# A gathered double-weight kernel: the first slot of x issued first, cond moved to ScalarE's queue, 2 MB of x ahead of the hold

## The reference

```python
def reference(x, subjects, conditions, weights0, weights1):
    x = x + einsum('bct,bcd->bdt', x, weights0[subjects])
    x = x + einsum('bct,bcd->bdt', x, weights1[conditions])
    return x
```

## Time and profile before

| What | Value |
|---|---|
| time, median of 3 runs | 92.88 us (92.86 to 92.94) |
| time of the profiled execution | 92.97 us |
| its span, first to last instruction | 91.2 us |
| TensorE busy (matmuls) | 79.2 us, 87% |
| VectorE, ScalarE busy | 61.8 us, 58.6 us |
| DMA moved | 35.93 MB, mean 394 GB/s |
| DMA queue q1 (SP's) | 33.56 MB, 91.5% of 16 engines |
| DMA queue q0 (the gather) | 2.10 MB, 5.4% |
| DMA queue q10 (ScalarE's) | 0.13 MB, 0.5% |

### The profile page before, as it was taken

The page is one execution under the profiler, slowest core; times in us unless marked ns, Lnnn a source line. Parts: engine busy times, 40 slices in busy tenths (PEclk is TensorE's granted clock), DMA queues, the critical chain, the costliest instruction groups (busy, mean ns, idle before and its releaser), DMA issues.

```text
span 91.2 us, 2427 instructions
## 1 busy us (share of the span) xinstructions
PE 79.2 (87%) x890; PEld 45.6 (50%) x890; DVE 61.8 (68%) x127; ACT 58.6 (64%) x117; POOL 23.4 (26%) x119
## 2 busy tenths in 40 slices
PE   0599979985999999999999999999999999999100
PEld 0488959974454544454454445445545444443000
DVE  1096009996287878787888787888778888788600
ACT  2899806886276776676777576777657676676500
POOL 3400039989999988000000000000000000000000
PEclk9999999999999999999999999999999999999955
DMA  0999999999999999999999999999999999999992
GB/s 12 335 438 422 453 361 420 411 406 415 406 408 408 406 408 413 415 394 417 408 403 415 420 419 420 410 424 415 419 415 419 415 422 422 419 419 404 417 404 104
DMA packets 9181, 35.93 MB, mean 394 GB/s; under 512 B 721, under 2 KB 850, under 8 KB 9042
## 3 DMA queue, kind: packets, MB, share of 16 engines
q1 hardware_dynamic: 8880, 33.56, 91.5%
q0 software_dynamic: 144, 2.10, 5.4%
q10 hardware_dynamic: 146, 0.13, 0.5%
HBM read 19.01 MB, written 16.78 MB: 392 GB/s over the span
## 4 chain that ended last, share of the span: by engine, by line
PE 70%; DMA 12%; DVE 9%; issue 1%; DVEq 1%; ACTq 0%; POOLq 0%
PE psum L229 62%; DMA w_rows<-in_L_cond_weights_dram,cond 10%; DVE w L248 7%; PE psum L210 7%; DMA subjects<-in_itok_B_dram 2%; DVEq L69 1%; DVE xy L270 1%; PE psum L190 1%; DVE m_diag L262 1%; ACTq L319 0%; DVE w_rows L314 0%; POOLq L159 0%; DVEq L254 0%
## 5 line engine op out<-in xcount | busy, mean ns | idle before, releaser
L229 PE MATMUL psum<-xy,m_diag 64*128 64x512 f32 x256 | 57.1, 595 | 0.5 <-DVE m_diag L262 0.5
L270 DVE COPY xy<-psum 64x512 f32<-64x512 f32 x64 | 43.7, 684 | 13.1 <-PE psum L229 12.1
L270 ACT COPY xy<-psum 64x512 f32<-64x512 f32 x64 | 37.2, 581 | 19.8 <-PE psum L229 19.0
L229 PEld LDWEIGHTS psum<-xy,m_diag 64*128 64x128 f32 x256 | 25.2, 187 | 26.7 <-issue 25.4
L167 POOL COPY w0b<-w0t 64x64 f32 x112 | 21.6, 235 | 10.1 <-DMA w_rows<-in_L_cond_weights_dram,cond 8.4
L210 PEld LDWEIGHTS psum<-w,w0b 64*32 64x32 f32 x512 | 5.6, 105 | 6.4 <-issue 3.8
L248 ACT COPY w<-psum 64x256 f32<-64x256 f32 x16 | 5.8, 364 | 4.0 <-PE psum L190 3.0
L180 PE MATMUL psum<-ident,w_rows 128*64 128x128 f32 x54 | 8.1, 326 | 0.0
L262 DVE TENSOR_SCALAR m_diag<-psum,mask 128x256 f32<-128x256 f32 (+1 forms) x18 | 7.2, 448 | 1.1 <-PE psum L210 0.9
L190 PE MATMUL psum<-ident,w_rows 128*64 128x128 f32 x64 | 7.2, 274 | 0.7 <-DVE w_rows L314 0.7
L327 ACT COPY w<-w_rows 128x256 f32<-128x256 f32 x18 | 7.3, 404 | 0.8 <-DMA w_rows<-in_L_cond_weights_dram 0.2
(11 more groups left out here) (8 smaller groups left out, 2.3 us busy)
## 6 DMA issues: line engine op xcount, KB each, us to landing
xy<-in_x_dram SPq DMA_DIRECT2D x15, 1024.0 KB, 18.5
out_dram<-xy SPq DMA_DIRECT2D x15, 1024.0 KB, 14.8
xy<-in_x_dram SPq DMA_DIRECT2D x2, 512.0 KB, 5.9
out_dram<-xy SPq DMA_DIRECT2D x2, 512.0 KB, 4.7
w_rows<-in_L_cond_weights_dram ACTq DMA_DIRECT2D x1, 128.0 KB, 2.5
cond<-in_itok_B_dram SPq DMA_DIRECT2D x1, 0.5 KB, 2.3
subjects<-in_itok_B_dram ACTq DMA_DIRECT2D x1, 0.5 KB
w_rows<-in_L_cond_weights_dram,cond POOLq DMA_INDIRECT x1, 9.3
```

What stands on the lines that cost most here:

```text
L229: last = nc.tensor.matmul(psum[:, 2 * (s % Y_RING) + h, :], m_diag[rows, odd, v % M_RING, j, :], xy[rows, s, j * T:(j + 1) * T], start=j = ...
L270: copy(xy[rows, s, i * T:(i + 1) * T], psum[HALVES[i], 2 * (s % Y_RING) + h, :]).then_inc(done, 1)
```

## The change

SP no longer issues cond. It issues slot 0 and slot 1 of x as two DMAs of 512 KB, then slots 2 and 3 as one of 1 MB, all ahead of the hold, so that 2 MB stand there and not 1.5 MB. cond is issued by ScalarE, ahead of w0. The count that TensorE waits for follows: unit 0 now has two DMAs, unit 1 one.

```diff
-            sp.dma_start(cond[:, :], cond_dram.rearrange("(b o) -> b o", o=1)).then_inc(s_cond, 16)
-            load(0, 2)
-            load(2, 1)
+            load(0, 1)
+            load(1, 1)
+            load(2, 2)
 
             sp.wait_ge(s_w0b_early, EARLY * UNIT)
-            load(3, 1)
             for v in range(2, UNITS):
                 load(2 * v, 2)
@@
-                    pe.wait_ge(s_x[v], 32 if v == 1 else 16)
+                    pe.wait_ge(s_x[v], 32 if v == 0 else 16)
@@
         def _(act):
+            act.dma_start(cond[:, :], cond_dram.rearrange("(b o) -> b o", o=1)).then_inc(s_cond, 16)
             act.dma_start(w0_rows[:, :, :], w0_dram.rearrange("s (k j) d -> (s k) j d", j=ROWS)
                           ).then_inc(s_w0_rows, 16)
```

## The result

The changed kernel takes 94.91 us (median of 6 runs, 94.44 to 95.73), the kernel before 93.01 us beside it: a ratio of 1.0212, with a 95% interval of 1.0182 to 1.0241. It is 2.1% slower. The forecast had the sign, and 93.35 us; the time lies 1.3 us above the forecast's own range (93.1 to 93.6) and 1.0 us above the range over the cases (up to 93.9).

A forecast was written before the change was run, and what follows sets the result against it. Bounds: TensorE's chain, then the DMA engines' queued stores. TensorE 2.0 us later, less the 1.5 us cushion, is +0.5 us, 0.45 with the small gain off: 93.35 us, range 93.1 to 93.6.

The forecast's parts named there:

- the sign: Whole kernel: slower, given a chance of 0.60, against 0.18 for same and 0.22 for faster.
- the range over the cases: Whole kernel's time over the forecast and all rivals: 92.5 to 93.9 us.
- The two bounds and the cushion: Kernel's end: TensorE's chain, then stores queued on the DMA engines; TensorE may end up to 1.5 us later for nothing.
- The rival of 0.9 us: Last stores: the cushion is only 0.9 us, making 94.0 us; chance 0.08.
- How the queues share the engines: DMA engines at the start: queues served in order of arrival, with no sharing packet by packet.
- The landing of w0: Start, ScalarE's queue: w0 lands behind slot 1 of x at 5.9 us, +2.65 us, delaying TensorE's warming transposes.
- 2 MB ahead of the hold: Before the gather: 512 KB more in front of it, so it comes 1.17 us later, at no cost to the engines.
- rival 1: w0 slips ahead of slot 1, D is the gather's 1.17 us, engines stay the bound: 92.45 to 92.7 us; chance 0.22.
- x 0.44 us sooner: Start, SP's queue: x issued 0.44 us sooner gains the engines 0 to 0.44 us, taken as 0.15.
- The hold: SP's wait before further loads of x: opens at 11.1 us, just covered by the gather, gap up to 0.2 us.
- Rival 2: Hold opens too late through subjects; engines run dry 0.5 to 1 us after the gather: 93.3 to 93.9 us; chance 0.13.

The follow-up runs named there:

- 12 rounds, early hold: Changed kernel with 12 warming rounds of TensorE for 18 and the hold opened by w0t, not the copies after it: 95.12 us, ratio 1.0183.

## Why the prediction was right or wrong

**The two bounds and the cushion:** right. TensorE's start carries through to its end (3.61 us at the start, 3.57 at the end), and the cushion was 1.5 by my reading and is 1.56. The rival of 0.9 us is out.

**How the queues share the engines:** this step failed. From the earlier trace rows I concluded "order of arrival, with no sharing packet by packet". In the changed kernel x and cond go one to one (54 and 54), and in the run with 2 MB alone x mixes with the gather's tail. It isn't wrong everywhere: with cond alone moved, w0 did wait for the load of x that had been issued first. The gather's rows couldn't show it: its packets are 16 KB, 8 per engine, and its descriptors may simply have been ready no earlier. The Trainium skill (DMA: Bandwidth & Descriptors, section Queues, rings and completion order) has the engines go round robin between rows, and typically puts 9 to 17 descriptors into a turn. The counts of the changed kernel bear out the round robin, with turns of one; the run with cond alone doesn't show it. A 4-byte packet in a turn costs 0.30 - 0.16 = 0.14 us, beside a recorded 8 ns (2.8% of 16 us, by 54). The Trainium skill (DMA: Bandwidth & Descriptors, section Specifications) says that below 512 B an engine reads, modifies and writes. That agrees with the price, and with w0's packets of 1 KB costing x nothing beyond their bytes, though no run here shows what the engine does in that time.

**The landing of w0,** the term that was mis-sized: 5.9 us forecast, 7.25 measured, so +4.0 us and not +2.65. The larger part is cond: it landed at 0.75 + 4.4 = 5.15 us, where I had 4.3 as the latest, because I gave its 4-byte packets no time of their own. w0 then needed 2.1 us more behind it, where I had 1.6. The warming stretch isn't a constant either: 8.55 us, not 8.10, as its pace doubled 0.9 us later after its start. With both, D is 3.55 and not 2.0, and the time 1.55 us above the forecast of 93.35: all of the miss by TensorE's bound.

**2 MB ahead of the hold:** also mis-sized, but hidden behind w0. I had the gather 1.17 us later and its addition by 14.0; it was 1.9 us later, at 14.60, and 2.0 us with the 2 MB alone. So with w0 in time D would still have been about 2, as in the run with 12 rounds (1.96), and not the 1.17 of rival 1. That the bytes ahead cost the engines nothing was right: with the 2 MB alone they have no debt.

**x 0.44 us sooner:** wrong in sign. I had a gain of 0 to 0.44 us, but bounded it only by w0's bytes. The 128 packets of cond, half a KB in all, halved x's rate for 2.5 us; by 7 us 0.50 MB are missing. Before, cond and most of w0 passed while next to none of x's bytes had come.

**The hold:** "just covered" forecast, with w0 at 5.9. It opened at 12.46 us, not 11.1, and a dip of 0.66 to 0.81 at 13.5 to 14.5 us followed. Rival 2 took part, by w0 and not by subjects as I had put it.

**The clock** wasn't in the prediction at all. In the changed kernel the granted clock stays at 1.00 once TensorE has begun with w1, but with the 2 MB alone or with w0 ahead of cond it falls, and costs 1.7 and 2.7 us.

So the changed kernel loses twice, 2.0 us by TensorE and 1.2 us by the engines, of which only the larger shows. A forecast with w0 in time would still have been too low: the engines' bound is 94.3 us, and taking TensorE's part back gave no gain. None of the kernels tried is faster than the one before.

## What to carry to other kernels

Count packets, not bytes, for what shares the DMA engines with a large stream: here 8 packets of 4 bytes per engine on a second queue cost what stood behind them a turn of the stream each. In the kernel before, which no other beat, the small transfers that gate the compute engines pass before the stream's first bytes arrive. Where two bounds lie within 1.5 us of each other, price an edit against both, and expect that mending one shows nothing. If TensorE is kept busy by a fixed number of rounds, any change that moves what ends the wait needs the number set again.

## What the runs showed of the hardware

- Two queues of the same 16 engines can take turns packet by packet, by the counts: 54 packets of 4 KB and 54 of 4 bytes in 1 us, 79 of 4 KB and 83 of 1 KB in another run. They don't always: with cond alone moved, w0 waited for nearly a whole DMA of x. What decides it is open. A turn with 4 bytes takes 0.30 us per engine, against 0.156 for 4 KB alone; with 1 KB the engines keep 399 GB/s.
- A stream of 4 KB packets that stops comes back at 90 and 262 GB/s in the two half microseconds before it is at its rate of 400 or so. With a gap of 1.5 us, the engines had moved 1.02 MB less by 16 us.
- TensorE idle for 3.29 us, having been busy at the full clock: the granted clock was still 1.00 in 15.0 to 16.3 us, when it had begun again, then 0.50 in 16.5 to 19.5 and 1.00 again from 20, which cost 1.66 us of D. After 3.85 us idle, with w0 ahead of cond, it was 0.50 in 16.5 to 23. After 1.45 us idle (12 rounds, early hold) it was 1.00 in 15.5 to 20, and after 0.65 us, in the kernel before, 1.00 in 13 to 20.
- A program with less work can spend more time outside the span of its instructions: 2.1 to 3.2 us with 12 warming rounds, against 1.8.
